# Two float32 halves in one matmul: the expert layers' second product at 512 columns

## The chip, the cores and the metric

The kernel runs on one core of a Trainium2 chip. The metric is the device time of one execution in microseconds, lower is better. A core has TensorE (PE: matrix products, which read SBUF and write to PSUM), VectorE (DVE), ScalarE (ACT), GpSimd (POOL) and SyncE (SP), each with its own queue; they order themselves by semaphores. PSUM has 8 banks here, of 128 partitions by 512 float32 numbers each.

## The reference

A graph of 2500 nodes with 256 features and 40,000 edges goes through a relational graph layer pair, a mixture of 8 experts, three plain graph layers with a projection, and a second mixture of 8 experts. Each part is added to its input. The change touches only the mixtures. Cut to that:

```python
for e in range(E):                                     # first mixture
    h = relu(einsum('bsd,hd->bsh', x, W1[e]) + b1[e])  # 256 -> 1024
    y = einsum('bsh,dh->bsd', h, W2[e]) + b2[e]        # 1024 -> 256
    out = out + combine[..., e:e + 1] * y              # two experts a node
# second mixture: the same with an affine norm per expert, exact gelu, and
# y = einsum('enh,ehd->end', h, W2) + b2[:, None, :]
```

## The kernel before, in words

Products of float32 numbers are made from two halves. A number is split into a high half of the type fp32r and a low half, the rest. A product is the sum of three matmuls: high by high, high by low and low by high. In `experts` the helper `products` issues these three into one PSUM region.

`experts(m, to)` runs twice, once for each mixture (m = 0 in the middle of the kernel, m = 1 at its end). The routing before it has sorted pairs of node and expert by expert, in MTILES = 47 tiles of 128 slots; each tile has one expert, read at run time from `texp`. The weights of four experts (RING) lie in the SBUF tensor `big`, named `ring` in the trace: first the high halves of four experts, then, RING x WE = 16,384 elements further on, the low halves. SyncE loads the experts 4 to 7 into a slot when the last tile of the expert there has had its y summed (`sp.wait_ge(y_summed, end)`, L2193), and TensorE waits for `expert_ready` (L2242) before a tile's first product.

For each tile:

- GpSimd gathers 128 rows of x, five tiles ahead (L2205).
- TensorE turns x (`turn_x`, L2231), and VectorE makes its halves (`take_x`, L2292 to L2298; in the second mixture with the expert's affine norm).
- TensorE computes h in two banks (`up`, 12 matmuls of 512 columns); VectorE adds the bias (`take_h`, L2313).
- TensorE turns h (`turn_h`, 8 transposes, L2255) into the banks psG. ScalarE applies relu or gelu to each bank twice, once to float32 and once to the high half (`take_g`, L2345 and L2346), and VectorE subtracts to get the low half (`take_low`, L2303).
- TensorE computes y in one of the two banks psY (`down`): 8 chunks of the hidden size, three matmuls of 256 columns each, 24 in all. Only columns 0 to 255 of the bank are used.
- VectorE adds the second bias to y (`take_y`, L2322) and signals `y_summed`. ScalarE scales by the routing weight (`scale_y`, L2353), and GpSimd adds the rows to the output by an indirect DMA (L2213). A scatter waits until the one before it has landed.

All matmuls of `up` and `down` have one source line in the trace, L2236.

The order is written out by hand. TensorE: `up(i)`, `turn_x(i + 1)`, `down(i - 1)`, `turn_h(i)`. VectorE: `take_h(i + 1)`, `take_x(i + 2)`, `take_y(i)`, `take_low(i + 1)`. ScalarE: `take_g(i + 1)`, `scale_y(i)`.

Of the kernel before, what the change touches and what calls it, by code (L numbers as in the profile page):

```python
# [11 lines left out]
F32R = mybir.dt.float32r  # L12
I32 = mybir.dt.int32
ALU = mybir.AluOpType
# [3 lines left out]
P = 128  # L18
NODES = 2500
D = 256  # L20
# [40 lines left out]
H = 1024  # L61
HC = H // P
# [5 lines left out]
W1E = KD * H  # L68
UNITW = KD * H
W2E = HC * D  # L70
WE = W1E + W2E
# [60 lines left out]
class Program:  # L132
# [2018 lines left out]
    def experts(self, m, to):  # L2151

        nc, a = self.nc, self.a
        affine = m == 1
        func = (ACT.Relu, ACT.Gelu)[m]
        psH, psX, psG, psY = self.ps[0:2], self.ps[2], self.ps[3:5], self.ps[5:7]
        with ExitStack() as memory, self.stage_block() as (block, sem):
            halves = self.scoped(memory, "halves", SLOTCOLS)
            hT_high, hT_low = (halves[:, k * H:(k + 1) * H].bitcast(F32R) for k in range(2))
            xT_high, xT_low = (halves[:, 2 * H + k * D:2 * H + (k + 1) * D].bitcast(F32R) for k in range(2))  # L2160
            h = self.scoped(memory, "whole", H)[:, :]

            rows = [self.x[:, s * D:(s + 1) * D] for s in range(XROWS + 4)]
            xin, ysum, yout = rows[0:XROWS], rows[XROWS:XROWS + 2], rows[XROWS + 2:]
# [6 lines left out]
            for s, g in enumerate(self.gathered[0:XROWS]):  # L2171
                g.base += 16 * len(range(s, MTILES, XROWS))

            x_turned, x_step, xT_ready, h_full, h_ready, h_turned, g_ready, hT_ready, y_full, y_summed, y_ready = sem(
                "x_turned", "x_step", "xT_ready", "h_full", "h_ready", "h_turned", "g_ready", "hT_ready", "y_full", "y_summed", "y_ready")
            expert_ready, refilled = sem("expert_ready", "refilled")
            x_steps = 3 if affine else 1

            def expert(eng, i):
# [1 line left out]

            def weights(slot, half, at, n):
                return self.big[:, bass.ds(slot * WE + (half * RING * WE + at), n)].bitcast(F32R)

            @block.sync
            def _(sp):
                for s in range(XROWS):
                    sp.wait_ge(x_in[s], x_before[s] + 16)
                sp.wait_ge(self.experts_late, 16 * (m + 1) * (RING // 2))
                sp.sem_inc(expert_ready, RING // 2)  # L2190
                for e in range(RING, E):
                    end = sp.value_load(self.texp[0:1, MTILES + e - RING:MTILES + e - RING + 1], min_val=1, max_val=MTILES + 1)
                    sp.wait_ge(y_summed, end)  # L2193
                    sp.sem_inc(self.gate, 1)
                    self.load_split(sp, e, m * (E - RING) + e - RING, refilled)
                    self.fetch_bias(sp, m, e, refilled)
                    sp.wait_ge(refilled, 32 * (e + 1 - RING))
                    sp.sem_inc(expert_ready, 1)
# [26 lines left out]
            @block.tensor  # L2225
            def _(pe):
                def turn_x(i):
                    s = i % XROWS
                    pe.wait_ge(x_in[s], x_before[s] + 16 * (i // XROWS + 1))
                    for k in range(KD):  # L2230
                        last = nc.tensor.transpose(psX[:, k * P:(k + 1) * P], xin[s][:, k * P:(k + 1) * P], self.ident[:, :])  # L2231
                    last.then_inc(x_turned, 1)

                def products(to, lhs, slot, at, n, first, last):
                    for left, right in ((0, 0), (0, 1), (1, 0)):
                        ins = nc.tensor.matmul(to, lhs[left], weights(slot, right, at, n), start=first and (left, right) == (0, 0),  # L2236
                                               stop=last and left == 1)
                    return ins

                def up(i, e):  # L2240
                    slot = e % RING
                    pe.wait_ge(expert_ready, e + 1)  # L2242
                    pe.sem_inc(self.gate, 1)
                    pe.wait_ge(xT_ready, i + 1)

                    for b in range(HB):
                        for k in range(KD):
                            last = products(psH[b][:, :], [x[:, k * P:(k + 1) * P] for x in (xT_high, xT_low)], slot,
                                            k * H + b * 512, 512, k == 0, k == KD - 1)
                    last.then_inc(h_full, 1)  # L2250

                def turn_h(i):
                    pe.wait_ge(h_ready, i + 1)
                    for c in range(HC):
                        last = nc.tensor.transpose(psG[c // 4][:, (c % 4) * P:(c % 4 + 1) * P], h[:, c * P:(c + 1) * P], self.ident[:, :])  # L2255
                    last.then_inc(h_turned, 1)

                def down(i, e):

                    slot = e % RING  # L2260
                    for c in range(HC):
                        if c % (HC // 2) == 0:
                            pe.wait_ge(hT_ready, i * 2 + (1 + c // (HC // 2)))
                        last = products(psY[i % 2][:, 0:D], [x[:, c * P:(c + 1) * P] for x in (hT_high, hT_low)], slot,
                                        W1E + c * D, D, c == 0, c == HC - 1)
                    last.then_inc(y_full, 1)

                pe.sem_inc(expert_ready, RING // 2)
                pe.sem_inc(y_full, 1)
                owner = [expert(pe, 0), expert(pe, 1)]  # L2270
                turn_x(0)
                up(0, owner[0])
                turn_x(1)
                turn_h(0)
                for i in range(1, MTILES):
                    up(i, owner[i % 2])
                    if i + 1 < MTILES:
                        turn_x(i + 1)
                    down(i - 1, owner[(i - 1) % 2])
                    if i + 1 < MTILES:  # L2280
                        owner[(i + 1) % 2] = expert(pe, i + 1)
                    turn_h(i)
                down(MTILES - 1, owner[(MTILES - 1) % 2])

            @block.vector
            def _(dve):
                def take_x(i):
                    e = expert(dve, i) if affine else None
                    dve.wait_ge(x_turned, i + 1)
                    if affine:  # L2290
                        for k in range(KD):
                            nc.vector.tensor_scalar(xT[:, k * P:(k + 1) * P], psX[:, k * P:(k + 1) * P], lng[:, bass.ds(e * KD + k, 1)],  # L2292
                                                    lnb[:, bass.ds(e * KD + k, 1)], ALU.mult, ALU.add).then_inc(x_step, 1)
                        dve.wait_ge(x_step, i * 3 + 2)
                    whole = xT if affine else psX[:, 0:D]
                    nc.vector.tensor_copy(xT_high, whole).then_inc(x_step, 1)  # L2296
                    dve.wait_ge(x_step, i * x_steps + x_steps)
                    nc.vector.tensor_tensor(xT_low, whole, xT_high, ALU.subtract).then_inc(xT_ready, 1)  # L2298

                def take_low(i):  # L2300
                    for b in range(2):
                        dve.wait_ge(g_ready, i * 2 + (b + 1))
                        nc.vector.tensor_tensor(hT_low[:, b * 512:(b + 1) * 512], hT[:, b * 512:(b + 1) * 512],  # L2303
                                                hT_high[:, b * 512:(b + 1) * 512], ALU.subtract).then_inc(hT_ready, 1)

                def bias(e, at, n):
                    return self.acc[:, bass.ds((e % RING) * BIASW + at, n)]

                def take_h(i):
                    e = expert(dve, i)  # L2310
                    dve.wait_ge(h_full, i + 1)
                    for b in range(HB):
                        last = nc.vector.tensor_tensor(h[:, b * 512:(b + 1) * 512], psH[b][:, :], bias(e, b * 512, 512), ALU.add)  # L2313
                    last.then_inc(h_ready, 1)

                def take_y(i):
                    e = expert(dve, i)
                    s = i % 2
                    if i >= 2:
                        dve.wait_ge(y_ready, i - 1)  # L2320
                    dve.wait_ge(y_full, i + 2)
                    nc.vector.tensor_tensor(ysum[s], psY[s][:, 0:D], bias(e, H, D), ALU.add).then_inc(y_summed, 1)  # L2322

                dve.sem_inc(y_summed, 1)
                take_x(0)
                take_h(0)
                take_x(1)
                take_low(0)
                for i in range(MTILES):
                    if i + 1 < MTILES:  # L2330
                        take_h(i + 1)
                    if i + 2 < MTILES:
                        take_x(i + 2)
                    take_y(i)
                    if i + 1 < MTILES:
                        take_low(i + 1)
# [60 lines left out]
```

## Time and profile before

| | |
|---|---|
| Median of 3 runs | 2281.48 us (2280.98 to 2284.77) |
| Span of the profiled execution | 2274.5 us (its time with what lies around the span isn't recorded) |
| TensorE busy | 1886.6 us, 83% of the span |
| VectorE busy | 1208.4 us, 53% |
| ScalarE busy | 1002.9 us, 44% |
| GpSimd busy | 943.2 us, 41% |
| First expert stage | from 1132.9 us, 327.7 us |
| Second expert stage | from 1932.9 us, 335.1 us |

The profile page has busy time by engine, and the other views used below take a stretch of the same execution: the timeline (instructions in order, merged, with the idle time before them and who ended it), the waits, the table by stretch, and the chain of waits that ended last. Times in a row are microseconds from the span's start, unless marked ns. A matmul's recorded duration holds its pipeline's end, so neighbours overlap; the distance from start to start is what one costs. PEld is TensorE's weight load, one for each matmul.

### The profile page before, as it was taken

How to read it: one execution, taken by the hardware profiler on the slowest of the kernel's cores; microseconds unless marked ns; L12 is line 12 of the kernel's file. 1: busy time of each engine (PE TensorE's matmuls, PEld its weight loads, DVE VectorE, ACT ScalarE, POOL GpSimd, SP SyncE). 2: the span in 40 equal slices, each digit the busy share in tenths (PEclk: the TensorE clock that was granted, in tenths of full speed). 3: DMA queues.
4: the chain of work that ended last, by engine and by line, in shares of the span. 5: the costliest groups of instructions: out<-in, count | busy, mean ns of one | idle time of the engine just before them, and what ended most of it. 6: DMA issues, size and time to landing. Idle time of an engine off the chain costs nothing. (4 is left out here: it accounts for less than half of the span.)

```text
span 2274.5 us, 37277 instructions
## 1 busy us (share of the span) xinstructions
PE 1886.6 (83%) x10428; PEld 1566.7 (69%) x10428; DVE 1208.4 (53%) x2759; ACT 1002.9 (44%) x2229; POOL 943.2 (41%) x877
## 2 busy tenths in 40 slices
PE   5996687788768878886499999579899864999997
PEld 3884476677645555554389999568688854899996
DVE  6331122122178879873555555465554565666664
ACT  1556465466365656653033333245444420233332
POOL 0115777777377777776033433220000000334332
PEclk9997899899989999998599999889999965999998
DMA  4895566665468656564535342347664556424262
GB/s 151 346 371 207 175 228 223 222 233 196 145 231 313 212 194 200 191 197 145 215 117 179 72 128 38 76 137 244 238 220 163 175 221 246 122 40 125 42 192 41
DMA packets 127195, 410.00 MB, mean 180 GB/s; under 512 B 21012, under 2 KB 60928, under 8 KB 108544
## 3 DMA queue, kind: packets, MB, share of 16 engines
q1 hardware_dynamic: 56848, 185.62, 22.2%
q0 software_dynamic: 48096, 106.74, 18.3%
q10 hardware_dynamic: 22032, 114.96, 13.4%
q8 instruction: 108, 1.77, 0.3%
q14 instruction: 111, 0.91, 0.1%
HBM read 256.77 MB, written 150.47 MB: 179 GB/s over the span
## 5 line engine op out<-in xcount | busy, mean ns | idle before, releaser
L2236 PE MATMUL ps<-ring,halves 128*128 x3384 | 578.8, 326 | 11.5 <-DVE halves L2303 4.0
L2236 PEld LDWEIGHTS ps<-ring,halves 128*128 128x128 f32 x3384 | 486.2, 192 | 53.8 <-issue 13.3
L1434 POOL DMA_INDIRECT ring<-tab_rel_next,gidx_relation x313 | 350.9, 1121 | 127.6 <-issue 93.9
L1126 POOL DMA_INDIRECT relation_rest<-tab_rel,gidx_relation x313 | 313.6, 1002 | 105.5 <-issue 94.5
L2345 ACT ACTIVATE x_all<-ps 128x512 f32<-128x512 f32 x188 | 113.0, 601 | 452.6 <-PE ps L2255 452.6
L1196 PE MATMUL ps<-relation_rest,slots 128*128 x784 | 214.9, 424 | 96.6 <-SPq L1041 96.2
L1526 PE MATMUL ps<-ring,slots 128*128 x784 | 202.8, 404 | 86.1 <-SPq L1311 59.5
L1893 PE MATMUL ps<-node_rows,blocks 128*128 128x512 f32 (+1 forms) x1200 | 258.5, 366 | 0.1
L1196 PEld LDWEIGHTS ps<-relation_rest,slots 128*128 128x128 f32 x784 | 161.8, 212 | 136.7 <-issue 110.0
L1526 PEld LDWEIGHTS ps<-ring,slots 128*128 128x128 f32 x784 | 147.7, 198 | 129.4 <-issue 111.0
L1893 PEld LDWEIGHTS ps<-node_rows,blocks 128*128 128x128 f32 x1200 | 203.2, 194 | 30.9 <-ACT blocks L1775 0.6
L2303 DVE TENSOR_TENSOR halves<-x_all,halves 128x512 fp32r<-128x512 f32 x188 | 130.3, 693 | 147.4 <-ACT halves L2346 147.4
L1141 DVE TENSOR_TENSOR acc<-acc,ps 128x257 f32 x98 | 41.4, 422 | 291.6 <-PE ps L1196 290.2
L1463 DVE TENSOR_SCALAR scratch<-ring,scratch,count_key 128x640 f16<-128x640 f16 x480 | 177.9, 440 | 0.0
L1537 PE MATMUL ps<-scratch,ring 128*128 128x320 f16 x960 | 155.8, 303 | 17.7 <-DVE scratch L1463 17.3
L2004 POOL IOTA x_all<- 128x20 f32 x2 | 0.3, 148 | 389.7 <-POOLq L206 389.7
L1219 PE MATMUL ps<-relation_halves 128*128 128x512 f32 (+1 forms) x600 | 157.3, 404 | 0.0
L2213 POOL DMA_INDIRECT out<-x_all,place_of_slot x47 | 74.9, 1594 | 197.4 <-ACT x_all L2353 161.0
L2213 POOL DMA_INDIRECT x_sum<-x_all,place_of_slot x47 | 74.7, 1590 | 190.4 <-ACT x_all L2353 145.2
L1092 ACT ACTIVATE slots<-iota,dst_in_bucket 128x128 f32<-128x128 f32 x392 | 124.3, 389 | 51.5 <-PE ps L1196 35.7
L1371 ACT ACTIVATE slots<-iota,dst_in_bucket 128x128 f32<-128x128 f32 x392 | 124.6, 394 | 50.8 <-issue 16.8
L2205 POOL DMA_INDIRECT x_all<-tab_node,token_of_slot x94 | 93.4, 993 | 117.2 <-POOLq L206 79.9
(281 smaller groups left out, 2770.5 us busy)
## 6 DMA issues: line engine op xcount, KB each, us to landing
ring<-split_weights SPq DMA_DIRECT2D x12, 4096.0 KB, 14.5
split_weights<-relation_rest ACTq DMA_DIRECT2D x32, 1024.0 KB, 7.1
slots<-tab_counts SPq DMA_DIRECT2D x40, 640.0 KB, 4.0
tab_rel<-relation_rest SPq DMA_DIRECT2D x20, 1024.0 KB, 5.3
tab_rel_next<-relation_rest ACTq DMA_DIRECT2D x20, 1024.0 KB, 4.7
relation_rest<-in_ffn_units ACTq DMA_DIRECT2D x16, 1024.0 KB, 5.7
split_weights<-ring ACTq DMA_DIRECT2D x16, 1024.0 KB
ring<-split_weights SPq DMA_DIRECT2D x8, 2048.0 KB, 22.8
```

The source lines that it names most:

```text
L1126: nc.gpsimd.indirect_dma_start(rows[:, s * wide:s * wide + D], None, table, bass.IndirectOffsetOnAxis(ap=gidx[:, t:t + 1], axis=0)).then_i ...
L1196: last = t.matmul(self.ps[g % BANKS][:, 0:wide], self.onehots[:, h * P:(h + 1) * P], rows[:, bass.ds((first + j) % RINGROWS * wide, wide)] ...
L1219: last = t.matmul(bank(n, width), self.row_halves[b % 2][left][:, k * P:(k + 1) * P], w[k][right], start=(k == 0 and left == right), stop= ...
L1371: last = nc.scalar.activation(to[:, j * P:(j + 1) * P], self.iota[:, 0:P], ACT.Square, scale=-1.0, bias=self.rel[:, g * GROUP + j:g * GROU ...
L1434: nc.gpsimd.indirect_dma_start(rows[:, s * D:(s + 1) * D], None, table, bass.IndirectOffsetOnAxis(ap=gidx[:, t:t + 1], axis=0)).then_inc(g ...
L1463: v.tensor_scalar(pair_hots[j], places, base[:, k:k + 1], self.key[:, bass.ds(at + j, 1)], ALU.add, ALU.is_equal).then_inc(pair_hot, 1)
L1526: last = t.matmul(self.ps[g % SUMBANKS][:, 0:D], self.onehots[:, h * P:(h + 1) * P], rows[:, bass.ds((first + j) % RINGROWS * D, D)], star ...
L1537: last = t.matmul(self.ps[BANKS + k % 2 * 2 + h][:, 0:half], src_hots[k % 2][:, j * P:(j + 1) * P], pair_hots[j][:, h * half:(h + 1) * hal ...
L1893: last = nc.tensor.matmul(to, self.blocks[b % 2][:, g * P:(g + 1) * P], self.node_tile(layer, g), start=False, stop=(g == TILES - 1))
L2213: nc.gpsimd.indirect_dma_start(to, bass.IndirectOffsetOnAxis(ap=self.place[:, i:i + 1], axis=0), yout[i % 2], None, compute_op=ALU.add).th ...
L2236: ins = nc.tensor.matmul(to, lhs[left], weights(slot, right, at, n), start=first and (left, right) == (0, 0), stop=last and left == 1)
L2303: nc.vector.tensor_tensor(hT_low[:, b * 512:(b + 1) * 512], hT[:, b * 512:(b + 1) * 512], hT_high[:, b * 512:(b + 1) * 512], ALU.subtract) ...
```

## The change

In `down`, the high half of the activation is multiplied by both halves of the second weights in one matmul of 512 columns: its moving operand is an access pattern of two runs of 256 elements, and its result fills the whole bank, high by high in columns 0 to 255 and high by low in columns 256 to 511. The low half of the activation is still multiplied by the high half of the weights, into columns 0 to 255. VectorE adds the two parts of the bank in a second operation of `take_y`, which waits for the first.

```diff
-            expert_ready, refilled = sem("expert_ready", "refilled")
+            expert_ready, refilled, y_step = sem("expert_ready", "refilled", "y_step")
...
+            def both_halves(slot, at, n):
+
+                by_half = self.big[:, :].rearrange("p (h w) -> p h w", h=2)
+                return by_half[:, :, bass.ds(slot * WE + at, n)].bitcast(F32R)
...
                     for c in range(HC):
                         if c % (HC // 2) == 0:
                             pe.wait_ge(hT_ready, i * 2 + (1 + c // (HC // 2)))
-                        last = products(psY[i % 2][:, 0:D], [x[:, c * P:(c + 1) * P] for x in (hT_high, hT_low)], slot,
-                                        W1E + c * D, D, c == 0, c == HC - 1)
+                        at = W1E + c * D
+                        if c:
+                            nc.tensor.matmul(psY[i % 2][:, 0:D], hT_low[:, c * P:(c + 1) * P], weights(slot, 0, at, D), start=False, stop=False)
+                        last = nc.tensor.matmul(psY[i % 2][:, 0:2 * D], hT_high[:, c * P:(c + 1) * P], both_halves(slot, at, D),
+                                                start=(c == 0), stop=(c == HC - 1))
+                        if c == 0:
+                            nc.tensor.matmul(psY[i % 2][:, 0:D], hT_low[:, c * P:(c + 1) * P], weights(slot, 0, at, D), start=False, stop=False)
                     last.then_inc(y_full, 1)
...
                     dve.wait_ge(y_full, i + 2)
-                    nc.vector.tensor_tensor(ysum[s], psY[s][:, 0:D], bias(e, H, D), ALU.add).then_inc(y_summed, 1)
+                    nc.vector.tensor_tensor(ysum[s], psY[s][:, 0:D], bias(e, H, D), ALU.add).then_inc(y_step, 1)
+                    dve.wait_ge(y_step, i + 1)
+                    nc.vector.tensor_tensor(ysum[s], ysum[s], psY[s][:, D:2 * D], ALU.add).then_inc(y_summed, 1)
```

## Rows read from the trace of the kernel before

**Rows 1.** The page, TensorE, VectorE and the others over the span.
```profile
PE 1886.6 (83%) x10428; PEld 1566.7 (69%) x10428; DVE 1208.4 (53%) x2759; ACT 1002.9 (44%) x2229; POOL 943.2 (41%) x877
```

**Rows 2.** Table by stretch: the two expert stages.
```profile
core 0: us, PE busy (x) PEld busy (x) DVE busy (x) ACT busy (x) POOL busy (x), PEclk, DMA share, GB/s
1132.90:1460.60 327.70, 319.20 (x2162) 291.79 (x2162) 181.28 (x329) 115.82 (x235) 119.15 (x92) 0.98 0.38 97
1932.90:2268.00 335.10, 321.54 (x2160) 293.95 (x2160) 210.42 (x423) 115.58 (x235) 118.76 (x91) 0.98 0.37 95
```

**Rows 3.** Timeline of a steady tile, TensorE: start, us, line, operands, count, idle before.
```profile
2093.68 3.11 PE L2236 MATMUL ps<-ring,halves 128*128 x24
...
2096.62 1.04 PE L2255 MATMUL ps<-ident,whole 128*128 128x128 f32 x8
...
2097.42 2.99 PE L2236 MATMUL ps<-ring,halves 128*128 x12
...
2100.25 0.38 PE L2231 MATMUL ps<-ident,x_all 128*128 128x128 f32 x2
...
2100.39 3.11 PE L2236 MATMUL ps<-ring,halves 128*128 x24
```

**Rows 4.** The same timeline, VectorE.
```profile
2097.28 0.42 DVE L2322 TENSOR_TENSOR x_all<-ps,acc 128x256 f32<-128x256 f32 x1 [0.46 <-PE ps L2236]
...
2098.82 0.69 DVE L2303 TENSOR_TENSOR halves<-x_all,halves 128x512 fp32r<-128x512 f32 x1 [1.11 <-ACT halves L2346]
...
2099.80 0.69 DVE L2303 TENSOR_TENSOR halves<-x_all,halves 128x512 fp32r<-128x512 f32 x1 [0.29 <-ACT halves L2346]
...
2100.62 1.29 DVE L2313 TENSOR_TENSOR whole<-ps,acc 128x512 f32<-128x512 f32 x2
...
2102.58 0.29 DVE L2296 CAST halves<-x_all 128x256 fp32r<-128x256 f32 x1
2102.91 0.42 DVE L2298 TENSOR_TENSOR halves<-x_all,halves 128x256 fp32r<-128x256 f32 x1
```

**Rows 5.** Waits of TensorE in the second stage: total us, times, longest.
```profile
PE ps L2236 <- SPq L2198: 3.9, 1, 3.9
```

**Rows 6.** Timeline, weight loads: within `down`, within `up` (two); the granted clock.
```profile
2101.42 1.63 PEld L2236 LDWEIGHTS ps<-ring,halves 128*128 128x128 f32 x13
...
2105.82 0.87 PEld L2236 LDWEIGHTS ps<-ring,halves 128*128 128x128 f32 x4
...
2104.44 1.34 PEld L2236 LDWEIGHTS ps<-ring,halves 128*128 128x128 f32 x6
...
2102.00:2103.00 1.00, 1.00 (x11) 1.00 (x10) 0.93 (x4) 0.00 (x0) 0.78 (x1) 1.00 0.05 16
```

**Rows 7.** Weight loads at the half clock: in `up`, in `down`; the granted clock.
```profile
1135.73 3.75 PEld L2236 LDWEIGHTS ps<-ring,halves 128*128 128x128 f32 x9
...
2260.61 2.68 PEld L2236 LDWEIGHTS ps<-ring,halves 128*128 128x128 f32 x12
...
2260.50:2263.80 3.30, 3.30 (x17) 3.30 (x17) 0.00 (x0) 0.00 (x0) 1.31 (x1) 0.50 0.35 40
```

**Rows 8.** Timeline, the end of the first stage: GpSimd's scatters, ScalarE's scaling.
```profile
1454.01 1.55 POOL L2213 DMA_INDIRECT x_sum<-x_all,place_of_slot  x1 [4.95 <-ACT x_all L2353]
...
1457.10 0.51 ACT L2353 ACTIVATE x_all<-x_all,weight_of_slot 128x256 f32<-128x256 f32 x1 [3.37 <-DVE x_all L2322]
1458.77 1.55 POOL L2213 DMA_INDIRECT x_sum<-x_all,place_of_slot  x1 [3.21 <-issue]
```

**Rows 9.** Timeline, the last `down` of the second stage.
```profile
2259.48 4.63 PE L2236 MATMUL ps<-ring,halves 128*128 x24 [1.99 <-DVE halves L2303]
```

**Rows 10.** The chain of waits at the last reload: start, us, what.
```profile
2201.23 2.88 PE ps L2236 x24
...
2205.84 16.09 DMA acc<-in_L_ffn_b
...
2222.30 4.61 PE ps L2236 x12
```

**Rows 11.** The line of `take_y`: duration ns min/median/max.
```profile
L2322 DVE TENSOR_TENSOR x_all<-ps,acc x94: 423/425/426, 1149.0 to 2264.4; 128x256 f32<-128x256 f32 x94
```

## The prediction

> **What bounds the kernel now.** I read the busy shares first, then the two stages that the change touches, the timeline of one tile, the waits, and last the chain of work. TensorE has 83% of the span [rows 1]. In the first expert stage it is busy for 319.20 of 327.70 us, in the second for 321.54 of 335.10, at a granted clock of 0.98; VectorE has 181.28 and 210.42 us there, ScalarE 116 in each [rows 2]. In a steady tile no TensorE line has an idle mark, and the period is 2100.39 - 2093.68 = 6.71 us: `down`, the turn of h, `up`, the turn of x [rows 3]. VectorE on the other hand waits for TensorE before it takes y (0.46 us) and for ScalarE before each low half (1.11 and 0.29 us) [rows 4]. So a nanosecond less in TensorE's products is one less in the period, until something else is late. TensorE's one long wait away from the start of a stage is that of 3.9 us for reloaded weights, in the second stage [rows 5]; it matters below.
>
> **The change part by part.**
>
> *TensorE.* In `down`, each of 8 hidden chunks has three products of 256 columns now (high by high, high by low, low by high), 24 a tile. After it there are 8 of 512 columns and 8 of 256, 16 a tile. The columns streamed stay 768 a chunk, so the gain can only be what a product costs beside its columns. Of 256 columns: 13 weight loads last 1.63 us, the last of them 0.19, so 12 steps take 1.44 us, 0.120 us each. Of 512 columns in `up`, with operands of the same types and the same weight memory: 4 loads in 0.87 us late in the piece, (0.87 - 0.19) / 3 = 0.227 us; 6 loads in 1.34 us earlier in it, 0.230 us [rows 6]. The forms differ by 0.107 us for 256 columns more, and that is 256 columns at 2.4 GHz, the clock granted there; so 0.013 us of each product is not columns. At the half clock this surcharge is absent: 9 loads of the 512 form in 3.75 us, with 0.33 for the last, are 0.427 us each, and 12 of the 256 form in 2.68 us are 0.214 [rows 7], exactly half, so there the change saves nothing.
>
> A chunk goes from 3 x 0.120 = 0.360 to 0.120 + 0.227 = 0.347 us, and 8 chunks save 0.104 us. A piece also pays a start: `down` takes 2096.62 - 2093.68 = 2.94 us against 24 x 0.120 = 2.88, so 0.06; `up` takes 2100.25 - 2097.42 = 2.83 against 12 x 0.227 = 2.72, so 0.11 [rows 3]. The new piece starts with a wide product but is half narrow, so its start lies between. With 0.06 the saving is 0.10 us a tile, with 0.11 it is 0.05. I take 0.08, a `down` of 2.86 us. With the 0.230 of the earlier part for all wide products it would be 0.03 at the least.
>
> How many of 47 tiles a stage keep it: in the first stage all but the last. The last scatter began at 1458.77, 1.16 us after ScalarE's scaling was over (1457.10 + 0.51) and 4.76 us after the scatter before it, whose landing it must await [rows 8]; that earlier scatter hangs on the last turn, not on the last `down`. In the second stage the last `down` ran mostly at the half clock, 4.63 us [rows 9]. And the chain leaves TensorE at the reload: from the end of a `down` at 2204.11 over VectorE's y, SyncE and the transfer to the restart at 2222.30 it is 18.2 us [rows 10]. TensorE's work beside it is 18.2 - 3.9 = 14.3 us, two periods and a turn, hence two `down`s, and shorter ones only lengthen the wait. That leaves 46 + 44 = 90 tiles, 90 x 0.08 = 7.2 us.
>
> What the trace can't show is the new moving operand: two runs of 256 columns, RING x WE = 16,384 elements apart; no row has such a product. The nearest rows bound it: nothing, if the second run follows like further columns; 0.013 us a product, if it costs what a product of its own costs, which takes back the whole 0.104; at the far end 0.427 - 0.227 = 0.20 us, if it streamed as slowly as at the half clock. Below nothing is excluded, as 512 columns are streamed in any case. I take nothing, since the nearest row is the wide product of `up`.
>
> The Trainium skill speaks against my surcharge: "TensorE: Matmul & The Clock Gate", section Back-to-back issue gap, has a product step as its columns over the clock plus 2.5 ns. By it the 8 dropped products are worth 0.02 us a tile, 90 x 0.02 = 1.8 us in all instead of 7.2. Rows 6 have 13 ns where it has 2.5, so the trace disagrees.
>
> *TensorE's register work.* The address computations of `down`, two a chunk now, one or two after, run ahead of the array, which shows no gap for them [rows 3]. Cost nothing; if that cover were gone, fewer of them would be a gain, so nothing is lost here.
>
> *VectorE.* A tile gets a second add of 128x256, the form of the one that is there, 0.425 us [rows 11], after a wait on the engine's own result. The nearest such wait is from the cast at 2102.58 (0.29 us long) to the subtraction at 2102.91: 0.04 us [rows 4]. So taking y grows by 0.465 us, 94 times, 44 us in all if nothing hid it. What hides it is the wait for ScalarE: y is over at 2097.70, with the second add at 2098.17, and the low half queued behind it starts at 2098.82, when ScalarE has delivered. 0.65 us stay. Behind that the next tile's h follows the second low half by 0.13 us (2100.49 to 2100.62), a distance that hangs on ScalarE and the turn, not on y. ScalarE scales y only after its fourth activation, which released the second low half at 2099.80, so the later sum delays neither it nor the scatter. VectorE's load in the second stage becomes 210.42 + 47 x 0.465 = 232 of some 331 us.
>
> That cover is missing at two places, where y itself is on the path: ahead of the reload, whose command starts 0.465 us later [rows 10], and at the very end, where the last scatter follows y and its scaling. Together +0.93 us. At the other reloads TensorE doesn't wait, and the end of the first stage has 1.16 us of cover.
>
> Sum: -7.2 + 0.9 = -6.3 us. The page gives the span of the profiled execution, 2274.5 us, and no other time of it; the span becomes 2268.2. The median of the runs, 2281.48, is 7.0 us above the span, for what lies around it, which I leave alone: 2275.2 us, 0.28% less. With 0.05 and 0.10 us a tile it is 2277.9 and 2273.4. The pieces at the half clock behind a wait (4.61 us for an `up` of 2.99, 4.63 for the last `down` against 3.11) are 1.5 us each; when everything shifts, one may go or another come, so 1.5 us more on either side.
>
> **The rivals.**
> (a) *No gain:* the second run costs about as much as a product of its own, or the surcharge goes with the columns. For it: the earlier part of `up` has 0.230, so a wide product can cost more than 0.227, and the two-run form is in no row. Against it: 0.120 and 0.227 fit one fixed surcharge, and at the half clock both forms are exact. Only the +0.9 us is left: 2282.4. By the skill's 2.5 ns (same page and section) it would be 2281.5 - 1.8 + 0.9 = 2280.6, no change either; rows 6 contradict that rule, and it has 0.04 of this rival's chance.
> (b) *Slower:* each jump between the runs breaks the stream, in all wide products of `down`. The tile's gain is gone at 0.013 us a jump, and the kernel is slower by over 0.2% (4.6 us) from (6.3 + 4.6) / 720 = 0.015 us, 90 x 8 = 720 products. At twice the surcharge, 0.027 us, it is 19.4 us: 2275.2 + 19.4 = 2294.6. For it: the restart after a turn costs tenths of a product (the 0.11 us of `up`), so the stream has a price of starting. Against it: both runs lie in one memory at fixed steps.
> (c) *More gain:* a narrow product is held by its weight load, not by its columns, and the load can now hide behind the wide product ahead of it. The narrow step falls from 0.120 to its columns, 0.107, another 720 x 0.013 = 9.4 us: 2265.8. Against it: the load would then hold the wide steps less too, and they show the same 0.013.
>
> **How the numbers follow.** Chances: forecast 0.63, (a) 0.22, (b) 0.10, (c) 0.05. The range is 2271 (0.10 us a tile and a half-clock piece gone) to 2283, which takes in (a). A measurement of this kernel tells a change from none at about 0.2%, 4.6 us, so faster means below 2276.9. The forecast's own range, 2272 to 2279.5, lies about four fifths below that: 0.63 x 0.8 + 0.05 of (c) is 0.55. Slower is (b), 0.10. The rest, 0.35, is no change: (a) and the upper fifth of the forecast.
>
> **What would show it.** 16 products in `down`, 2.86 us from its first start to the turn, a period near 6.63 us; narrow steps of 0.120, wide ones of 0.227 to 0.230 us; two adds of 0.425 us for y with 0.04 between, and still an idle mark by ScalarE before the low half; a wait for the reload of about 4.5 us instead of 3.9. I am wrong if the wide step of `down` is above 0.24 us (a, b), if the narrow step falls (c), or if TensorE shows idle time before `down` or the turn of h that VectorE ends.

## The result

The changed kernel takes 2271.26 us (median of 13 runs) against 2279.45 us before (13 runs): the ratio is 0.9965, with an interval of 0.9953 to 0.9976, so 8 us less, between 5.5 and 10.7. Two later comparisons of the same two programs gave 0.9976 (0.9961 to 0.9990) and 0.9964 (0.9951 to 0.9977). The forecast was 6.3 us less. A ratio here isn't that of the two medians; where both are given below, they differ by up to 2 us. One of the 25 runs of the kernel before in the first later comparison was in a slow state (2368.84 us, granted clock 0.80) and has no part in any ratio. The span of the profiled execution is 2269.2 us, 5.3 below that of before.

The page after, first part: TensorE has 752 fewer products and the same share of the span, and VectorE is 40 us busier for its 94 more adds.

```profile
span 2269.2 us, 35115 instructions
...
PE 1883.3 (83%) x9676; PEld 1525.6 (67%) x9676; DVE 1248.6 (55%) x2853; ACT 1003.6 (44%) x2229; POOL 943.6 (42%) x877
```

One steady tile of the second stage, TensorE's timeline of the changed kernel. L2260 is the turn of h, L2241 `up`, L2236 the turn of x, L2272 a wide product of `down`, L2271 and L2275 a narrow one.

```profile
2093.00 1.04 PE L2260 MATMUL ps<-ident,whole 128*128 128x128 f32 x8
2093.79 3.00 PE L2241 MATMUL ps<-ring,halves 128*128 x12
2096.63 0.38 PE L2236 MATMUL ps<-ident,x_all 128*128 128x128 f32 x2
2096.76 0.48 PE L2272 MATMUL ps<-ring,halves 128*128 x1
2097.08 0.28 PE L2275 MATMUL ps<-ring,halves 128*128 x1
2097.20 0.28 PE L2271 MATMUL ps<-ring,halves 128*128 x1
2097.32 0.40 PE L2272 MATMUL ps<-ring,halves 128*128 x1
2097.55 0.28 PE L2271 MATMUL ps<-ring,halves 128*128 x1
...
2098.02 0.40 PE L2272 MATMUL ps<-ring,halves 128*128 x1
2098.25 0.28 PE L2271 MATMUL ps<-ring,halves 128*128 x1
...
2099.64 0.49 PE L2260 MATMUL ps<-ident,whole 128*128 128x128 f32 x3
```

There is still no idle mark. The period is 2099.64 - 2093.00 = 6.64 us (6.71 in [rows 3]), `down` 2099.64 - 2096.76 = 2.88 (2.94). A wide step is 2097.55 - 2097.32 = 0.23, and two chunks are 2098.02 - 2097.32 = 0.70 us, 0.35 each, as the step sizes of [rows 6] say.

The same view in the first stage gives something else:

```profile
1277.84 1.04 PE L2260 MATMUL ps<-ident,whole 128*128 128x128 f32 x8
1278.63 3.01 PE L2241 MATMUL ps<-ring,halves 128*128 x12
1281.49 0.38 PE L2236 MATMUL ps<-ident,x_all 128*128 128x128 f32 x2
1281.62 0.48 PE L2272 MATMUL ps<-ring,halves 128*128 x1
...
1282.52 0.40 PE L2272 MATMUL ps<-ring,halves 128*128 x1
1282.76 0.28 PE L2271 MATMUL ps<-ring,halves 128*128 x1
1282.88 0.40 PE L2272 MATMUL ps<-ring,halves 128*128 x1
...
1284.53 0.71 PE L2260 MATMUL ps<-ident,whole 128*128 128x128 f32 x5
```

Here the period is 6.69 us: a wide step is 0.24, `down` takes 2.91 us, and even `up`, which the change doesn't touch, is 1281.49 - 1278.63 = 2.86 instead of 2.83. Both stages hold their own period without change from the second tile on, but for the last tile and the one at the last reload (6.687 us on average here, 6.640 in the second, against 6.707 before in both). The gain of a tile is 0.020 us in one stage and 0.067 in the other.

VectorE in the second stage, in answer to [rows 4]: the timeline around y. The two adds are 0.42 us with 2094.00 - (2093.54 + 0.42) = 0.04 between, and the low half behind them still waits 0.77 us for ScalarE.

```profile
2093.54 0.42 DVE L2332 TENSOR_TENSOR x_all<-ps,acc 128x256 f32<-128x256 f32 x1 [0.47 <-PE ps L2272]
...
2094.00 0.42 DVE L2334 TENSOR_TENSOR x_all<-x_all,ps 128x256 f32<-128x256 f32 x1
...
2095.19 0.73 DVE L2313 TENSOR_TENSOR halves<-x_all,halves 128x512 fp32r<-128x512 f32 x1 [0.77 <-ACT halves L2358]
```

The chain of waits at the last reload, in answer to [rows 10]: both adds lie in it, but the transfer took 14.89 us instead of 16.09.

```profile
2199.99 0.44 DVE x_all L2332
...
2200.45 0.43 DVE x_all L2334
...
2200.99 0.53 SPq L1940
...
2201.90 14.89 DMA acc<-in_L_ffn_b
...
2217.15 5.48 PE ps L2241 x12
```

TensorE's waits there, in answer to [rows 5]: 3.6 us.

```profile
PE ps L2241 <- SPq L2203: 3.6, 1, 3.6
```

### The profile page after: what moved, and what is told of

The parts are those of the page before. It is cut to its first block and busy times, and to the rows that moved or that the text cites. A ratio compares the mean times of both kernels' runs of the same rounds, so it can differ in the third digit from the quotient of the medians.

```text
span 2269.2 us, 35115 instructions
## 1 busy us (share of the span) xinstructions
PE 1883.3 (83%) x9676; PEld 1525.6 (67%) x9676; DVE 1248.6 (55%) x2853; ACT 1003.6 (44%) x2229; POOL 943.6 (42%) x877
## 5 line engine op out<-in xcount | busy, mean ns | idle before, releaser
L2241 PE MATMUL ps<-ring,halves 128*128 x1128 | 288.0, 405 | 7.3 <-DVE halves L2308 3.7
L2272 PE MATMUL ps<-ring,halves 128*128 x752 | 281.4, 408 | 4.0 <-DVE halves L2313 4.0
L2241 PEld LDWEIGHTS ps<-ring,halves 128*128 128x128 f32 x1128 | 208.7, 192 | 49.8 <-issue 8.5
L2271 PE MATMUL ps<-ring,halves 128*128 x658 | 184.8, 281 | 0.0
L2272 PEld LDWEIGHTS ps<-ring,halves 128*128 128x128 f32 x752 | 142.4, 189 | 30.4 <-issue 4.4
```

What stands on the lines that cost most here:

```text
L2271: nc.tensor.matmul(psY[i % 2][:, 0:D], hT_low[:, c * P:(c + 1) * P], weights(slot, 0, at, D), start=False, stop=False)
L2272: last = nc.tensor.matmul(psY[i % 2][:, 0:2 * D], hT_high[:, c * P:(c + 1) * P], both_halves(slot, at, D), start=(c == 0), stop=(c == HC - 1))
```

## The experiments

Three questions were open: whether a stage is bound to its period or falls into it by chance, what VectorE's second add costs, and whether the two-run operand (a wide product's two runs of 256 columns) costs anything. Ratios are against the kernel before, with a 95% interval; the microseconds beside a ratio are worked out from it. A run that was "measured once" has no interval, and only its profile is used.

### The changed kernel again

No edit.

> The changed kernel once more, beside the kernel before. The first pair of profiles has a tile period of 6.687 us in the first expert stage (6.707 before) and 6.640 in the second (6.707 before), so 45 x 0.020 + 42 x 0.067 = 3.7 us of steady gain. Theory A: the two periods are two fixed rhythms of TensorE, each tied to its stage; this run shows 6.687 and 6.640 again, and the time is 5 to 9 us below before (ratio 0.9965). Theory B: a stage falls into a rhythm by chance in each execution; then at least one stage shows another period here, and the times of the changed kernel spread by about 2 to 3 us more than those of before.

Measured: 0.9976 (0.9961 to 0.9990), 5.5 us less. Stage 1 had 6.687 us a tile, stage 2 6.640, the same as in the first pair. The reload waited 3.8 us. Alone this speaks for theory A (each period tied to its stage); the next run and a third run of this same program, further below, go against it. The times spread from 2269.5 to 2285.2 us, those of the kernel before from 2275.6 to 2287.0, so the wider spread of theory B isn't clear.

### One add

```diff
-                    nc.vector.tensor_tensor(ysum[s], psY[s][:, 0:D], bias(e, H, D), ALU.add).then_inc(y_step, 1)
-                    dve.wait_ge(y_step, i + 1)
-                    nc.vector.tensor_tensor(ysum[s], ysum[s], psY[s][:, D:2 * D], ALU.add).then_inc(y_summed, 1)
+                    nc.vector.tensor_tensor(ysum[s], psY[s][:, 0:D], bias(e, H, D), ALU.add).then_inc(y_summed, 1)
```

> VectorE's second add is left out (the part of y that the low half of the weights gives is not in the output). Theory of the prediction: it is hidden beside TensorE except at the reload and the end, so the time is 0.9 us below the changed kernel, the tile periods are the same, and the wait for the reload is 0.46 us shorter. Rival: the added operation also sets TensorE's rhythm or delays the low half somewhere; then a period changes by 10 ns or more, and the time by 2 us or more.

Measured: 0.9967 (0.9955 to 0.9978), 7.5 us less than before. Against the changed kernel of the same session it is 1.4 us less by the medians (2272.06 and 2273.44), but the intervals overlap, so the time doesn't show the 0.9 us. What the profile shows is the exchange of the periods: 6.640 in the first stage, 6.687 in the second. The turns of h, in both:

```profile
1273.06 1.04 PE L2260 MATMUL ps<-ident,whole 128*128 128x128 f32 x8
1279.70 1.04 PE L2260 MATMUL ps<-ident,whole 128*128 128x128 f32 x8
...
2071.42 1.04 PE L2260 MATMUL ps<-ident,whole 128*128 128x128 f32 x8
2078.11 1.04 PE L2260 MATMUL ps<-ident,whole 128*128 128x128 f32 x8
```

6.64 and 6.69 us. So neither period belongs to a stage. A period did change by more than 10 ns, the mark of the rival, but one went down and the other up, and the third run of the unchanged program shows such a change without any edit. The wait for the reload was 2.8 us: y comes 0.46 us earlier, and its transfer took 14.61.

One thing more differs there. `up` behind this wait took 3.00 us at a granted clock of 1.00; in the changed kernel, behind a wait of 3.6 us, it took 5.48 us at 0.50 (chain above).

```profile
2215.66 3.00 PE ps L2241 x12
```

So the profiled execution of this run is 2.5 us shorter there for its clock alone. In the other profiles `up` took 4.5 to 5.5 us behind waits of 3.0 us and more.

### The kernel before with two operations on y

```diff
-                    nc.vector.tensor_tensor(ysum[s], psY[s][:, 0:D], bias(e, H, D), ALU.add).then_inc(y_summed, 1)
+                    nc.vector.tensor_tensor(ysum[s], psY[s][:, 0:D], bias(e, H, D), ALU.add).then_inc(y_step, 1)
+                    dve.wait_ge(y_step, i + 1)
+                    nc.vector.tensor_tensor(ysum[s], psY[s][:, 0:D], bias(e, H, D), ALU.add).then_inc(y_summed, 1)
```

> The kernel before, with only VectorE's part of the change: y is taken twice, the second time with the same result. Theory: the tile period stays 6.707 us in both stages and the time is 0.9 us above before (ratio 1.0004), the 0.46 us at the reload and at the end. Rival: y is longer on the path than two places, and the time is 3 us or more above before.

Measured: 0.9998 (0.9987 to 1.0009). 0.9 us more lies in the interval, 3 us more doesn't. The period is 6.707 us in both stages: 94 operations of 0.425 us, 40 us of VectorE's time, cost the steady tile nothing. The wait at the reload is 4.7 us, which alone says little, for the two profiles of the kernel before have 3.9 and 4.9, with transfers of 16.09 and 17.05. The distance from the start of y's first operation to the start of the transfer says it: 2206.98 - 2205.07 = 1.91 us here against 2205.84 - 2204.40 = 1.44 in the kernel before, 0.47 more. The kernel before, then this one:

```profile
2204.40 0.44 DVE x_all L2322
...
2205.84 16.09 DMA acc<-in_L_ffn_b
```

```profile
2205.07 0.44 DVE x_all L2322
...
2205.53 0.44 DVE x_all L2324
...
2206.98 16.42 DMA acc<-in_L_ffn_b
```

### The second mixture without the affine norm

```diff
-        affine = m == 1
+        affine = False
```

> The changed kernel, the second mixture without the experts' affine norm: its two operations of 128x128 on VectorE are left out for each tile, so x is ready 0.6 us earlier, as in the first mixture. Theory A1: the slower rhythm of the first stage comes from when VectorE's x releases TensorE's queue; then the second stage here has the period of the first, 6.687 us instead of 6.640. Theory A2: the rhythm comes from something else (the stage's place in the program, the clock's phase); then it stays at 6.640.

Measured once: 2267.51 us. Both stages had 6.640 us a tile, so the earlier x did not bring the slower rhythm, and A1 falls; the first stage, which the edit doesn't touch, had 6.640 here too. A2 had 6.640 right, but the exchange in the run with one add speaks against a place in the program as well.

### Four wide, four narrow

The loop over the chunks in `down` is replaced by this one:

```diff
...
+                    for b in range(2):
+                        chunks = range(b * (HC // 2), (b + 1) * (HC // 2))
+                        pe.wait_ge(hT_ready, i * 2 + (1 + b))
+                        for c in chunks:
+                            nc.tensor.matmul(psY[i % 2][:, 0:2 * D], hT_high[:, c * P:(c + 1) * P], both_halves(slot, W1E + c * D, D),
+                                             start=(c == 0), stop=False)
+                        for c in chunks:
+                            last = nc.tensor.matmul(psY[i % 2][:, 0:D], hT_low[:, c * P:(c + 1) * P], weights(slot, 0, W1E + c * D, D),
+                                                    start=False, stop=(c == HC - 1))
...
```

> The changed kernel with another order of the same 16 products in each tile: four wide ones (512 columns), four narrow ones (256), four wide, four narrow. Four profiles of the changed form so far show two rhythms, 6.640 and 6.687 us a tile, in either stage. Theory (surcharge per product, and the slow rhythm is bred by the alternation of wide and narrow): products of one width in a row run at 0.227 and 0.120 us as in the kernel before, both stages have one and the same period of 6.62 to 6.65 us, and the time is that of the changed kernel in its better rhythm, about 2270 us (ratio 0.9965). Rival (a wide product with two runs costs more than one of up, whatever its order): the wide steps in a row are 0.232 us or more, and the period is 6.66 us or above.

Measured: 0.9973 (0.9961 to 0.9985), 6.1 us less. One period of 6.640 us in both stages. TensorE's timeline, first stage (L2270 wide, L2273 narrow):

```profile
1272.11 1.04 PE L2260 MATMUL ps<-ident,whole 128*128 128x128 f32 x8
1272.90 3.00 PE L2241 MATMUL ps<-ring,halves 128*128 x12
1275.74 0.38 PE L2236 MATMUL ps<-ident,x_all 128*128 128x128 f32 x2
1275.87 1.18 PE L2270 MATMUL ps<-ring,halves 128*128 x4
1276.89 0.63 PE L2273 MATMUL ps<-ring,halves 128*128 x4
1277.36 1.08 PE L2270 MATMUL ps<-ring,halves 128*128 x4
1278.28 0.64 PE L2273 MATMUL ps<-ring,halves 128*128 x4
1278.75 0.49 PE L2260 MATMUL ps<-ident,whole 128*128 128x128 f32 x3
```

The last four wide and four narrow take 1278.75 - 1277.36 = 1.39 us, 0.35 a pair, the forecast's 0.347; the first eight take 1.49, the start of the piece included. `up` takes 2.84 us, as in the faster rhythm. In time this order isn't shown to differ from the changed kernel's (0.9973 against 0.9965, 0.9976 and 0.9964, with intervals that overlap).

### One run of 512 adjacent columns

The wide products read the high weights of two neighbouring chunks, so the products with the low weights are replaced.

```diff
-                        last = nc.tensor.matmul(psY[i % 2][:, 0:2 * D], hT_high[:, c * P:(c + 1) * P], both_halves(slot, at, D),
+                        last = nc.tensor.matmul(psY[i % 2][:, 0:2 * D], hT_high[:, c * P:(c + 1) * P], weights(slot, 0, W1E + min(c, HC - 2) * D, 2 * D),
```

> The changed kernel, but the wide products read 512 adjacent columns of the high weights instead of two runs of 256 (so y has the products with the low halves replaced by others). Theory: the two runs cost nothing; the period of each stage is again 6.640 or 6.687 us. Rival: the jump between the runs costs 3 to 9 ns a wide product, which the steps of 0.231 to 0.241 us hide; then the period falls by 0.02 to 0.07 us below 6.640, to 6.57 to 6.62 us.

Measured once: 2276.43 us, in which the tile with the last reload's wait took 20.2 us against 9.7 to 14.7 in the other profiles, so the time says nothing here. The wait comes one tile later than in every other profile, and TensorE has one period of work beside the transfer instead of two. The wrong y of the first mixture changes what the second one routes, which would explain it; no run shows that. The turns of h are what was asked for: 1279.06 - 1272.42 = 6.64 and 2075.59 - 2068.90 = 6.69 us.

```profile
1272.42 1.04 PE L2260 MATMUL ps<-ident,whole 128*128 128x128 f32 x8
...
1279.06 0.38 PE L2260 MATMUL ps<-ident,whole 128*128 128x128 f32 x2
...
2068.90 1.04 PE L2260 MATMUL ps<-ident,whole 128*128 128x128 f32 x8
...
2075.59 0.38 PE L2260 MATMUL ps<-ident,whole 128*128 128x128 f32 x2
```

The same two values as with two runs. Wide products also step alike: behind the first one, seven take 0.233 us each on average in the stage at 6.640 us, here and in the changed kernel. The jump of 16,384 elements costs nothing, and the two rhythms don't come from it.

### Sixteen narrow products

```diff
-                        last = products(psY[i % 2][:, 0:D], [x[:, c * P:(c + 1) * P] for x in (hT_high, hT_low)], slot,
-                                        W1E + c * D, D, c == 0, c == HC - 1)
+                        for left, x in ((0, hT_high), (1, hT_low)):
+                            last = nc.tensor.matmul(psY[i % 2][:, 0:D], x[:, c * P:(c + 1) * P], weights(slot, 0, W1E + c * D, D),
+                                                    start=(c == 0 and left == 0), stop=(c == HC - 1 and left == 1))
```

> The kernel before without the products of the high activation half with the low weights (left out of y): 16 products of 256 columns a tile instead of 24. It prices a product where nothing else changes. Theory (columns plus 13 ns): the period falls by 8 x 0.120 = 0.96 us, from 6.707 to 5.75 us, and against this kernel the changed one pays 0.89 to 0.94 us for 8 x 256 columns more in the same number of products, 0.111 to 0.117 us for 256 columns (0.107 at the full clock). Rival: another engine sets the period before that (VectorE's chain through both low halves, h and x); then TensorE shows idle marks in the steady tile and the period stays above 5.8 us.

Measured once: 2211.43 us. In the first stage the period is 5.747 us, exactly 0.960 less, so a narrow product is worth 0.120 us. The changed kernel's 6.640 is 0.893 above it: 0.112 us for 256 more columns, in the range given. In the second stage the rival comes true as well: the period varies, mostly between 6.1 and 6.3 us. Its timeline:

```profile
2041.65 1.03 PE L2255 MATMUL ps<-ident,whole 128*128 128x128 f32 x8
2041.85 0.29 DVE L2297 CAST halves<-x_all 128x256 fp32r<-128x256 f32 x1
2042.18 0.43 DVE L2299 TENSOR_TENSOR halves<-x_all,halves 128x256 fp32r<-128x256 f32 x1
...
2042.79 2.60 PEld L2236 LDWEIGHTS ps<-ring,halves 128*128 128x128 f32 x12 [0.35 <-issue]
```

`up` now has to wait: x's halves are ready at 2042.61, and its first weight load follows at 2042.79 after 0.35 us of idle time. The row puts no engine to this idle time, but the waits of TensorE between 1900 and 2190 us have 20 waits of `up` for x's low half (L2299), 6.0 us in all. That is where VectorE's cover ends: some 6.1 to 6.3 us a tile in the stage with the affine norm.

### Wide first in every chunk

```diff
-                        if c:
-                            nc.tensor.matmul(psY[i % 2][:, 0:D], hT_low[:, c * P:(c + 1) * P], weights(slot, 0, at, D), start=False, stop=False)
...
+                        last = nc.tensor.matmul(psY[i % 2][:, 0:D], hT_low[:, c * P:(c + 1) * P], weights(slot, 0, at, D), start=False, stop=(c == HC - 1))
```

> The changed kernel with wide before narrow in every chunk (it has narrow before wide from the second chunk on), so the last product of a tile is narrow. Theory (the rhythm is bred by alternation): both periods are possible here too, 6.64 and 6.69 us or near them, in either stage, and the time is within 0.1% of the changed kernel's. Rival (the pair of two narrow products after the first wide one sets the rhythm): with the pair gone both stages have one period.

Measured: 0.9971 (0.9960 to 0.9983), 6.6 us less. A third period, 6.667 us, in both stages. That is what the rival said (one period with the pair gone). But one profile doesn't settle it: with the changed order too, both stages have the same period in two of six profiles. So it isn't shown that alternation alone doesn't breed two rhythms. Whether the pair of narrow products breeds the two rhythms stays open; all forms that showed two have it.

### The grouped order with an earlier reload

On top of the grouped order:

```diff
-                    sp.wait_ge(y_summed, end)
+                    sp.wait_ge(y_step, end)
...
-                    dve.wait_ge(y_step, i + 1)
+                    dve.wait_ge(y_step, i + 2)
...
+                dve.sem_inc(y_step, 1)
                 dve.sem_inc(y_summed, 1)
```

> The grouped order, and the reload of an expert's weights starts after VectorE's first operation on y (the one that reads the bias) instead of the second. Theory: both stages at 6.640 us a tile; at the last reload TensorE waits 0.46 us less than it would, the rest as grouped, so 6.0 to 7.5 us below before (ratio 0.9970). It beats the changed kernel where that one falls into its slower rhythm, by 0 to 4 us, 1 to 2 us in the median. Rival: what the rhythm costs is too little to be seen in the median, and the two kernels differ by less than 1 us.

Measured: 2268.96 us against 2280.28 us before, 0.9957 (0.9942 to 0.9973), 9.8 us less. It has the lowest ratio of the programs that compute all of y, with 6.640 us in both stages and a wait of 3.0 us at the reload (3.6 in the grouped order without it). Of the 0.6 us, 0.46 is the edit's: from y's first operation to the start of the transfer it is 1.44 us instead of 1.90. Against the changed kernel of the same session, below, it has the lower median by 5.1 us, but the two intervals overlap. It beats the kernel before; that it beats the changed one is not shown.

### The changed kernel a third time, and the kernel before once more

> The changed kernel a third time, on the chip that runs the grouped one. Theory (each stage of each execution falls into one of two rhythms): each stage shows exactly 6.640 or 6.687 us a tile, and no third value. The time is 5.5 to 8 us below before (ratio 0.9970). Rival (the first stage is bound to 6.687 and the second to 6.640, as in two profiles of this very program): 6.687 and 6.640 a third time.

> The kernel before once more, for its profile. Theory: it has one rhythm, 6.707 us a tile in both stages, as in the first profile and in the one with two adds, and its last reload lands 16 us after the issue. Rival: this form has a second rhythm too, which three stages out of four didn't show; then a stage has another period.

Measured: the changed kernel took 2274.07 us against 2280.28, 0.9964 (0.9951 to 0.9977), with 6.640 us in both stages. Its first stage:

```profile
1273.84 1.04 PE L2260 MATMUL ps<-ident,whole 128*128 128x128 f32 x8
...
1280.48 1.04 PE L2260 MATMUL ps<-ident,whole 128*128 128x128 f32 x8
```

So the same program had 6.687 in its first stage twice and 6.640 once: the rhythm is settled anew in each execution, theory B. No third value came. The kernel before had 6.707 in both stages, 2279.71 us in its one run, and its last reload landed after 17.05 us, one more than expected; the wait there was 4.9 us.

## Why the prediction was right

The side and the size held: 6.3 us less was forecast, the ratios of the three comparisons give 8.0, 5.5 and 8.2 us less (the medians 8.2, 6.3 and 6.2), and all three intervals contain 6.3 us. The mechanism held too, but that the sum came out so near is in part luck: the steady tiles gave less than forecast, and other places more.

- *What bounds.* TensorE had no idle mark in a steady tile before, and none after. Right; 40 us more on VectorE did nothing to it (two adds).
- *The surcharge of 0.013 us a product.* Right where it could be isolated: a narrow product is worth 0.120 us (sixteen narrow), and a wide and a narrow one in a row 0.347 (grouped). It isn't one fixed price, though: wide products in `down` step by 0.233 us on average behind the first, with adjacent columns too, and narrow ones among them by 0.116. The Trainium skill's 2.5 ns ("TensorE: Matmul & The Clock Gate", section Back-to-back issue gap) would have given 0.02 us a tile; the runs show 0.067 in all four stages with the grouped order.
- *0.08 us a tile.* This term was mis-sized. It is 0.067 us at best, and 0.020 us in the slower rhythm, which I did not have at all. What I called the start of `down` is 0.10 us now instead of 0.06, nearer to the bound of 0.05 than I took. But it isn't in the first product: that one costs 0.314 - 0.227 = 0.087 us more than a steady step now, and cost 0.203 - 0.120 = 0.083 before. It is in the wide steps behind it, 7 x 0.006 = 0.04 us over 0.227, of which the narrow steps of 0.116 give 8 x 0.004 = 0.03 back; before, the early narrow steps of 0.117 to 0.121 gave back 0.02 (means of some 20 tiles of the second stage). Over the steady tiles (45 and 44 periods) the kernel before took 596.5 us, the changed one 592.6, 592.6 and 590.5 in three profiles: 3.9, 3.9 and 6.0 us, not 7.2.
- *The two-run operand.* I took nothing, and it is nothing (one run). Rivals (a) and (b) fall as mechanisms; the slow rhythm did make wide steps of 0.24, the mark that I had set for them, without being theirs. (c) falls too: the narrow step stays near 0.120 (0.116 on average where it follows wide ones), not at 0.107.
- *VectorE's add.* 0.46 us each, hidden in the steady tile, and 0.47 us on the path to the reload's transfer (two operations). Right; the other 0.46 us, at the very end, no comparison isolates. The cover left in front of the low half was 0.77 us, 0.65 forecast.
- *The reload's wait.* 4.5 us was forecast; it was 3.6, 3.8 and 3.9 us. The forecast held the transfer at 16.1 us; it took 14.89, 15.31 and 15.18 us in the changed kernel, and 16.09, 17.05 and 16.42 in three profiles with 24 products. The step failed on a duration that I had taken as fixed. Why the transfer is shorter is open: eight of nine profiles of forms with wide products have 14.6 to 15.3 us, but the one with adjacent columns has 16.37, and the one with sixteen narrow products 16.69. Nor is 3.9 us the wait of the kernel before in general: its second profile has 4.9.
- *The lost tiles and the median.* I left 7.0 us around the span. Some 1.9 us lie there (2271.12 against 2269.2 in the profiled execution of the changed kernel); the rest was the distance of one execution to the median of others: the times of before reach from 2275 to 2285 us, and the profiled execution was a short one. For the difference it didn't matter. For the time itself it did, in part: 2275.2 us was forecast and 2271.26 measured, near the lower end of my range, and 2.0 us of the 3.9 lie in the median of before, 2279.45 beside the 2281.48 that I started from.
- *The chances.* I put about four fifths of the range 2272 to 2279.5 below 2276.9. By length it is 4.9 of 7.5, two thirds; four fifths holds only if the middle weighs more, which the prediction doesn't say.

The measured gain is more than the steady part. From first to last matmul start the two stages together took 654.9 and 657.0 us before, and 649.8, 649.2 and 646.5 after: on average 7.5 us less, of which the steady tiles give 4.6. The other 2.9 us lie before the first turn of h in each stage (0.9 us), in each stage's first period (0.1), at the reload (0.6) and behind the last turn (1.35). Most of these places have pieces that run at the half clock or don't. The last `down` of a stage is one: it takes 4.63 us at the half clock and 3.13 at the full one before, 4.61 and 3.04 after. Both profiles of before have one such `down`, in different stages, and of the three of the changed kernel only one has. The run with two operations on y, whose TensorE work is that of before, has none. So with two and three profiles, what of the 2.9 us belongs to the change (the reload's transfer may) and what is chance stays open.

## What to carry to other kernels

In a stage that TensorE fills, count what a product costs beside its columns, from two shapes of the same types in the trace, at the granted clock in question: here it was 0.013 us for each fp32r product at the full clock and nothing at the half clock. Joining two products into one of twice the width saves that once, if the engine that then has to add the parts has idle time behind a wait of its own. Expect less than the count says: of 0.104 us a tile 0.067 were left, or 0.020. It may pay to order products of one width in runs: the same 16 products gave 6.640 us a tile in all four stages when grouped, and 6.640 in eight and 6.687 in four when mixed. Four stages can agree by luck, and the time of the kernel doesn't show the difference.

## What the runs showed of the hardware that was not expected

- Two stable rhythms of one instruction stream. With the order wide, narrow, narrow, wide, narrow, wide and so on, a stage runs at 6.640 or at 6.687 us a tile from its second tile to its last but one, except where it waits for a reload. In six profiles with this order (twelve stages) eight had the first and four the second, and the products of `up` are slower with it too (2.85 us instead of 2.84). What sets it is open; it is neither the stage, nor when x is ready, nor the two-run operand. The other orders showed one value each: wide first 6.667 (two stages), grouped 6.640 (four), and three narrow ones a chunk 6.707 (six).
- A moving operand of two runs of 256 columns, 64 KB apart in a partition, streams like 512 adjacent ones (6.640 and 6.687 us a tile with either).
- The first product of 512 columns behind the transposes steps by 0.314 us and the first of 256 by 0.203, both about 0.085 us over their steady step.
